# Intermediate scratch laid out by expert with a padded pitch: 1 KB writes, 4 KB reads by half-tile transfers

## The reference

```python
grouped = x.reshape(B, S // t, t, D)                      # groups of 16 tokens
cont_logits = einsum('bgtd,des->bgtes', grouped, controller)
cont_perm = (cont_logits + tie == max over t)             # one-hot: one token of 16 per expert slot
intermediate = einsum('bgtd,desf->bgtesf', grouped, f1)
inner = relu(einsum('bgtesf,bgtes->bgesf', intermediate, cont_perm))
inter2 = einsum('bgesf,esfd->bgesd', inner, f2)
result = einsum('bgesd,bgtes->bgtd', inter2, cont_perm)   # every slot's product goes back to its token
```

## Time and profile before

| what | us |
|---|---|
| median of 3 runs | 817.79 |
| the profiled execution | 816.2 |
| its span, first to last instruction | 814.4 |
| attention, up to the first select | about 545 |
| experts of one chunk | about 23 |
| units with selects alone (chunk 0) | about 25 |
| units with scatters of the chunk before | about 37 |

### The profile page before, as it was taken

How to read it: one execution, slowest core, us unless ns; L and a number is a source line. 1 busy time by engine, 2 the same in 40 slices (tenths; PEclk the granted TensorE clock), 3 DMA queues, 4 the chain that set the end, 5 groups by cost and what they waited for, 6 DMA issues and landing times.

```text
span 814.4 us, 22451 instructions
## 1 busy us (share of the span) xinstructions
PE 736.0 (90%) x7252; PEld 561.0 (69%) x7252; DVE 612.7 (75%) x2558; ACT 568.5 (70%) x1654; POOL 125.5 (15%) x125
## 2 busy tenths in 40 slices
PE   4799999999999999999999999887988978986925
PEld 3578888888888888888888888665644655543602
DVE  2598998998998998988988988777655655654512
ACT  3499899899889899999999998745543543542400
POOL 1101000100100100010010006137234144100000
PEclk9899999999999999999999999899999999997956
DMA  5476566666656756765765664910789888888889
GB/s 155 109 181 148 134 164 155 145 149 155 160 135 155 172 131 147 171 146 132 171 154 125 148 149 106 261 51 2 316 310 303 338 310 289 353 297 275 332 303 304
DMA packets 102197, 157.60 MB, mean 194 GB/s; under 512 B 12288, under 2 KB 65024, under 8 KB 101888
## 3 DMA queue, kind: packets, MB, share of 16 engines
q1 hardware_dynamic: 99968, 155.56, 66.9%
q10 hardware_dynamic: 2176, 1.31, 0.7%
HBM read 47.78 MB, written 41.94 MB: 110 GB/s over the span
## 4 chain that ended last, share of the span: by engine, by line
PE 73%; DMA 15%; SPq 4%; DVE 4%; issue 2%; ACT 1%; ACTq 0%; DVEq 0%
PE bank L503 13%; PE bank L455 13%; DMA stage<-scratch 9%; PE bank L517 7%; PE bank L490 7%; PE bank L477 6%; PE bank L540 6%; PE bank L684 6%; PE bank L663 4%; SPq L301 3%; DMA XRlast<-scratch 2%; PE bank L448 2%; DMA scratch<-stage 2%; PE bank L531 2%; PE bank L652 2%
## 5 line engine op out<-in xcount | busy, mean ns | idle before, releaser
L828 ACT ACTIVATE Ps<-Ps,nmax 128x256 f32<-128x256 f32 x512 | 255.4, 503 | 24.9 <-DVE nmax L1017 23.2
L1017 DVE CUSTOM_DVE_ANT_0 Ps<-bank,masks 128x256 f32<-128x256 f32 x512 | 199.1, 420 | 27.4 <-issue 25.6
L503 PE MATMUL bank<-ident,Ps 128*128 128x128 f32 x1024 | 146.6, 276 | 2.0 <-DVE PTs L1028 1.5
L503 PEld LDWEIGHTS bank<-ident,Ps 128*128 128x128 f32 x1024 | 116.5, 141 | 20.3 <-issue 11.9
L455 PE MATMUL bank<-hT,WT 128*128 128x256 f32 x512 | 124.7, 388 | 0.8 <-ACT hT L785 0.8
L490 PE MATMUL bank<-stack 128*128 128x256 f32 x512 | 118.8, 334 | 5.5 <-DMA stack<-parts 5.4
L384 POOL TENSOR_TENSOR X<-X,bob 128x512 f32 (+1 forms) x32 | 40.8, 1277 | 430.0 <-ACT hn L793 430.0
L455 PEld LDWEIGHTS bank<-hT,WT 128*128 128x128 f32 x512 | 95.2, 195 | 12.1 <-issue 1.1
L828 ACT ACTIVATION_READ_ACCUMULATOR Ps<-Ps,nmax 128x1 f32 x512 | 98.2, 192 | 0.0
L396 POOL TENSOR_SCALAR h<-X,mv,roots 128x256 f32<-128x256 f32 x64 | 80.1, 1263 | 117.0 <-PE bank L652 89.2
L1028 DVE COPY PTs<-bank 128x512 f32<-128x512 f32 x128 | 87.7, 685 | 5.1 <-PE bank L503 5.0
(11 more groups left out here) (84 smaller groups left out, 1039.0 us busy)
## 6 DMA issues: line engine op xcount, KB each, us to landing
stack<-parts SPq DMA_DIRECT2D x512, 128.0 KB, 2.4
scratch<-stage SPq DMA_DIRECT2D x64, 512.0 KB, 4.1
stage<-scratch SPq DMA_DIRECT2D x48, 512.0 KB, 6.8
X<-in_x SPq DMA_DIRECT2D x32, 256.0 KB, 2.8
out<-X SPq DMA_DIRECT2D x32, 256.0 KB, 6.7
XRlast<-scratch SPq DMA_DIRECT2D x4, 2048.0 KB, 16.0
f1s<-in_L_ffn_f SPq DMA_DIRECT2D x1, 2048.0 KB, 8.1
f2s<-in_L_ffn_f SPq DMA_DIRECT2D x1, 2048.0 KB, 13.4
```

What stands on the lines that cost most here:

```text
L503: last = nc.tensor.transpose(PTb[h % 2][:, k * N + t * P:k * N + t * P + P], Ps[:, pr % 2, t, h % 2, k * P:k * P + P], ident[:, :])
L828: last = nc.scalar.activation(Ps[:, pr % 2, t, h, :], Ps[:, pr % 2, t, h, :], ACT.Exp, bias=nmax[:, pr % 2, t, h:h + 1], scale=-1.0, accum ...
L1017: last = nc.vector.tensor_tensor_reduce(out=Ps[:, pr % 2, t, h, :], in0=s_bank(n)[:, h * N:h * N + N], in1=masks[:, t, :], scale=1.0, scal ...
```

## The change

The scratch tensor changes from (group, slot x D) to (chunk, slot, group x D + 1024 values of padding). Slots are then 33,792 values, 132 KB, apart. A move writes, from each partition (group), four runs of 1 KB, one for each slot. Group order inside a chunk changes from "group, parity" to "parity, group" at the copy into XS, so that the four groups of one parity of a tile lie together: a gather reads one run of 4 KB for each slot and parity. It does so by two DMAs of 64 partitions, the first for partitions 0 to 63 and the second for 64 to 127. For the last chunk they are eight DMAs of 64 partitions with runs of 16 KB. Counts of semaphores double where two transfers stand for one.

```diff
-    scratch = nc.dram_tensor("scratch", (CHUNKS * CG, ES * D), F32, kind="Internal").ap()
+    PAD = 1024
+    scratch = nc.dram_tensor("scratch", (CHUNKS, ES, CG * D + PAD), F32, kind="Internal").ap()
     def by_group(c, q):
-        rows = slice(c * CG, c * CG + CG) if isinstance(c, int) else bass.ds(c * CG, CG)
-        return scratch[rows, 4 * q * D:4 * (q + 1) * D]
-
-    def by_expert(c, tile):
-        first = c * CG + GPT * tile
-        rows = slice(first, first + GPT) if isinstance(c, int) else bass.ds(first, GPT)
-        return scratch[rows, :].rearrange("(c two) (e d) -> (two e) c d", two=2, d=D)
+        return scratch[c, 4 * q:4 * q + 4, 0:CG * D].rearrange("e (p d) -> p e d", d=D)
+
+    def by_expert(c, tile, two, tiles=1):
+        first = (two * CP + GPT // 2 * tile) * D
+        return scratch[c, :, first:first + GPT // 2 * tiles * D]
...
-            first = GPT * tile + 4 * hf
-            return copy(XS[:, :, :, first:first + 4].rearrange("p k e (j two) -> p k e j two", two=2),
+            first = GPT // 2 * tile + 2 * hf
+            return copy(XS[:, :, :, :].rearrange("p k e (two c) -> p k e c two", two=2)[:, :, :, first:first + 2, :],
...
-                sp.dma_start(by_group(c, q), stage[:, q % SLOTS, :, :].rearrange("p j d -> p (j d)"))\
+                sp.dma_start(by_group(c, q), stage[:, q % SLOTS, :, :])\
...
-                sp.dma_start(XR[:, tile % SLOTS, :, :], by_expert(c, tile)).then_inc(gathered[tile % SLOTS], 16)
+                for two in range(2):
+                    sp.dma_start(XR[64 * two:64 * two + 64, tile % SLOTS, :, :].rearrange("p c d -> p (c d)"),
+                                 by_expert(c, tile, two)).then_inc(gathered[tile % SLOTS], 16)
...
-                rows = slice((CHUNKS - 1) * CG + 4 * GPT * i, (CHUNKS - 1) * CG + 4 * GPT * (i + 1))
-                sp.dma_start(XRlast[:, 4 * i:4 * i + 4, :, :].rearrange("p t j d -> p (t j) d"),
-                             scratch[rows, :].rearrange("(c two) (e d) -> (two e) c d", two=2, d=D))\
-                    .then_inc(last_in[i], 16)
+                for two in range(2):
+                    sp.dma_start(XRlast[64 * two:64 * two + 64, 4 * i:4 * i + 4, :, :].rearrange("p t j d -> p (t j d)"),
+                                 by_expert(CHUNKS - 1, 4 * i, two, 4)).then_inc(last_in[i], 16)
...
-                    pe.wait_ge(last_in[s // 2], 16)
+                    pe.wait_ge(last_in[s // 2], 32)
...
-                    pe.wait_ge(gathered[tile % SLOTS], landed(c, tile))
+                    pe.wait_ge(gathered[tile % SLOTS], 2 * landed(c, tile))
```

## The result

The changed kernel takes 883.25 us (median of 4 runs, 879.47 to 884.68) against 817.04 for the kernel before beside it (813.77 to 818.42): a ratio of 1.0817, 95% interval 1.0788 to 1.0846. It is 66 us slower. The forecast was 864 with a range of 808 to 882: the direction was right, and the time is 19 us above the forecast and 1 us above the range. The profiled execution took 883.18 us, its span is 881.4.

The account below looks back on a forecast made before the run. PE was taken to bound the experts, DMA the stretches with gathers and the last read. 816.2 + 1 (moves) + 49.2 (halves) - 4 (cover) = 862.4, plus 1.6 to the median: 864.0 us, range 808 to 882.

Parts of the forecast that it names:

- What bounds the kernel: From 570 us on: PE sets the pace of the experts, DMA that of the selects with scatters and last read.
- Halves: Gathers and last read: 64-partition transfers pass at 231 GB/s instead of 350, +12.3 us a chunk, +49.2 in all.
- The cover: Second stretch of gathers: PE was last for about 4 us, hiding added DMA time there, -4 us.
- Rival A: Reads: halves share nothing that matters and pass at about 400 GB/s, -11 us, 807; chance 0.19.
- B: Reads: paired engines drift into different halves half of the time, 315 GB/s, +11 us, 829; chance 0.14.
- Copies to XS: Selects: neighbours 64 elements apart in XS cost 0, copies stay at 697 ns; at most +10 us.
- Moves: Experts: writes in 1 KB runs pass at the stores' 383 GB/s, +1 us in all; bounds 0 and +10.
- rival C: Experts: 1 KB writes 132 KB apart bind, experts exceed 24 us, +9 us at 350 GB/s; 0.05 together with Rival A.
- Long runs: Reads: 4 KB runs alone are a gain, from 350 towards 400 GB/s; at 400, -3.0 us a chunk.
- PE's clock: More waiting brings 1.2 GHz in more places, but PE is mostly not last there: 0, bound +4 us.
- Range: Whole kernel: 808, the edge of Rival A, to 882, the forecast's upper bound; some 0.05 above it.

Follow-up runs that it names:

- e5: Kernel before with each gather and last read cut into two transfers, partitions 0 to 63 and 64 to 127: 870.69 us, ratio 1.0661.
- e10: Changed kernel with whole reads of 128 partitions, copies to XS reordered in pairs, and moves in 4 KB runs: 811.67 us, ratio 0.9919.
- e2: Changed kernel with each gather and last read as one transfer of 128 partitions instead of two of 64: 841.64 us, ratio 1.0346.
- e7: Kernel before with each gather and last read cut into two transfers over all 128 partitions, half of the runs each: 818.44 us, ratio 1.0031.
- e8: Kernel before with each gather and last read cut into two transfers, even and odd partitions: 823.26 us, ratio 1.0085.
- e6: Kernel before with only the copies to XS in the changed group order, neighbours 64 elements apart: 837.23 us, ratio 1.0284.
- e1: Changed kernel with copies to XS walking the same elements in another order, neighbours side by side in pairs: 867.82 us, ratio 1.0664.
- e9: Changed kernel with whole reads of 128 partitions and copies to XS reordered in pairs; moves stay in 1 KB runs: 825.0 us, ratio 1.0088.
- e4: Changed kernel with the second halves of the last chunk's reads issued on ACT's queue instead of SP's: 882.37 us, ratio 1.0795.

## Why the prediction was off, point by point

- **What bounds the kernel** held in the main: e5 makes the reads slower and e10 faster, and all four stretches follow. But the stretches with scatters had more room than was taken off (see halves), and were not DMA's alone (see copies).
- **Halves**: the forecast's main term, 4 x 12.3 less 4, 45 us, for the step from whole reads in short runs to halves in long ones. That a half is slow is shown (e2, e5, e7, e8), but the term was too large. Against whole reads in long runs the halves cost 38 us (e2); less the 6.6 that long runs gain (e10) it is about 32, not 45. The last read grew by 15.1 us where 12.3 was given, since 16 KB runs pass at 210 GB/s and not at 231. The three stretches grew by 9.3, 9.6 and 10.4, copies and all. The cover was taken off in the second alone, and the three grew alike; they do in e5 too, whose copies are fast, by 11.6, 11.3 and 11.7 beside the last read's 18.4. So 13 us too much here hid part of what the next two terms lacked; that is luck. Without it the forecast would have been near 851, an estimate from these differences, each of them uncertain by some 5 us. Rival A, no effect, is excluded; B, engines drifting apart, may stand behind the stretches moving 246 GB/s with their stores where the last read moves 213, but that was not tested.
- **Copies to XS**: the step that failed. It was set to nothing because the read side was already scattered and cost 12 ns. That row shows the cost of jumps on the PSUM side only; the writes lay four together in it. Jumps on the write side add some 610 ns to 697 on DVE and 720 to 590 on ACT (e6; e1 takes 570 and 580 of them away). The bound of +10 is what chunk 0 lost (+9.7), but "little where DMA is the bound" was wrong too: e6 shows 1 to 4 us in each stretch, where PE then waits 8.4 us for the copies and 3.5 for gathers. In all 12.5 to 23 us (e1, e6).
- **Moves**: set to +1, by the stores' 383 GB/s. They pass at 328, slower even than the 350 of the 1 KB reads that stood as the bound. That makes 6.7 us here and 14 from e9 to e10. So rival C held beside the forecast, with its sign that the experts take longer (12.7 us more in the four chunks). What stores have over moves was not tested; a store's rows follow each other in HBM, a move's are 132 KB apart for the four slots.
- **Long runs**: as forecast, near 400 GB/s and over (412 in e2). Their gain is 6.6 us in e10 where 12 would follow from four chunks of 3 us: the last read gained 2.8, the stretches with scatters 1.0 to 1.8 each.
- **PE's clock**, left at 0 with a bound of +4: behind chunk 0's selects, in which PE was busy 21.3 of 35 us, it ran the first quads of the experts at a granted clock of 0.50 (580 to 585.4 us), 1.2 GHz, where it was 1.00 before. The first expansion took 1.93 us instead of 1.08, and this chunk's experts 2 us more than the other three. That the slow copies are the cause isn't shown: e5 and e10, with faster ones, start at 1.94 too.
- **Range**: each cost had its upper bound written down, +10 for the copies and +10 for the moves, but the upper end, 882, took less than the two together beside the 864. By e6 the copies passed theirs, and the moves took 7 to 14 of their 10: 883.25.

## What to carry to other kernels

In these runs a transfer was as fast as the partitions it touches were spread: don't cut a tile at partition 64 where the queue is the bound; cut it by columns (e7), or by even and odd partitions (e8) if the queue can bear two issues of 0.6 us, and look at the bytes moved at a full DMA share, not at the share. Where a copy permutes, write out the order in which it walks the destination, and keep neighbours side by side at least in pairs; a row that shows jumps on the read side says nothing of the write side. Moving short runs from the read to the write only pays if the writes have room: here a move in runs of 4 KB took 1.30 us at a full share against PE's 1.35, in runs of 1 KB 1.54 to 1.60, and a gain of 7 us would have cost 14.

## What the runs showed of the hardware that I had not expected

- Copies of 512 fp32 from PSUM to SBUF on DVE and ACT: about 697 and 590 ns with four neighbours together in the destination, 741 and 729 with two, 1309 and 1312 where each neighbour lies some 256 bytes from the last.
- Halves of the partitions on two queues in parallel move 231 GB/s, little more than on one (210), and far from the 412 of whole transfers in the same runs (e4, e2).
- A half in runs of 1 KB passes at 194 GB/s and in runs of 16 KB at 210; the quarter in the earlier trace rows, from which I took one rate for both, at 231.
- Reads of every second partition pass at the rate of whole ones (346 against 350 GB/s). But a move or gather of 64 partitions took SP about 0.6 us to issue (median), neighbours or every second, where one over all 128 took 0.32 to 0.57.
